# Attention with a gated linear branch and a routed feed-forward layer: softmax weights normalised over four heads at once in the first two chunks of each group

## The reference, cut to what matters

```
scores = jnp.einsum('bqhd,bkhd->bhqk', sq, sk) * scale
scores = jnp.where(causal[None, None], scores, jnp.finfo(scores.dtype).min)
attn = jax.nn.softmax(scores, axis=-1)
y = jnp.einsum('bhqk,bkhd->bqhd', attn, sv)
o = 0.5 * y + 0.5 * o_gla
```

## Time and profile before

| what | us |
|---|---|
| median of three unprofiled runs (lowest, highest) | 944.18 (944.08, 945.03) |
| the profiled execution | 935.75 |
| its span, first to last instruction | 933.5 |
| TensorE matmul busy | 895.2 |
| TensorE weight load busy | 706.8 |
| VectorE busy | 679.4 |
| ScalarE busy | 663.2 |
| GpSimd busy | 635.4 |

### The profile page before, as it was taken

One profiled execution on the slowest core, in us unless ns is written; L12 is line 12 of the kernel. 1 busy time (PEld: TensorE's weight loads), 2 busy tenths in 40 slices (PEclk: granted clock), 3 DMA queues, 4 the chain that ended last, 5 costly groups with the idle time before them and its releaser, 6 DMA issues.

```text
span 933.5 us, 18329 instructions
## 1 busy us (share of the span) xinstructions
PE 895.2 (96%) x5145; PEld 706.8 (76%) x5145; DVE 679.4 (73%) x2010; ACT 663.2 (71%) x2147; POOL 635.4 (68%) x603
## 2 busy tenths in 40 slices
PE   7899999999999999999999999999999989799996
PEld 4577878777777777778788878787776766598885
DVE  5877877676767676767676978877888967475457
ACT  6687777777777777777686877778767767354656
POOL 6967676767566666768676767877656898546441
PEclk9999999999999999999999999999999999999999
DMA  7100100000000000620000001000003111125355
GB/s 266 35 12 29 29 24 1 6 13 7 1 0 0 0 0 7 178 62 1 1 1 2 1 1 44 1 1 17 17 17 106 40 61 41 57 86 148 109 149 202
DMA packets 30969, 41.46 MB, mean 44 GB/s; under 512 B 3230, under 2 KB 25631, under 8 KB 30624
## 3 DMA queue, kind: packets, MB, share of 16 engines
q1 hardware_dynamic: 27472, 31.98, 11.4%
q0 software_dynamic: 3408, 8.43, 2.5%
HBM read 24.72 MB, written 16.59 MB: 44 GB/s over the span
## 4 chain that ended last, share of the span: by engine, by line
PE 77%; DVE 9%; ACT 5%; POOL 4%; issue 3%; DMA 1%; DVEq 0%; POOLq 0%; ACTq 0%
PE PR L518 12%; PE OA L631 12%; PE S L585 10%; PE MS L604 8%; PE S L613 7%; PE OA L593 5%; PE OA L624 4%; PE S L731 3%; PE OA L748 3%; PE PR L564 3%; PE PR L558 3%; POOL slot_x L1717 1%; ACT eqk L879 1%; PE MS L547 1%; DVE pr L1111 1%
## 5 line engine op out<-in xcount | busy, mean ns | idle before, releaser
L1644 POOL TENSOR_TENSOR qd<-eqk,eg 128x512 f32<-128x512 f32 x63 | 75.0, 1190 | 132.3 <-issue 127.6
L631 PE MATMUL OA<-wT,V 128*128 128x512 f32 x320 | 148.4, 594 | 0.0
L841 ACT ACTIVATE S<-S,nm 128x128 f32<-128x128 f32 (+3 forms) x256 | 126.4, 494 | 6.6 <-DVE nm L1077 5.8
L1077 DVE CUSTOM_DVE_ANT_0 S<-S,maskb 128x128 f32<-128x128 f32 (+3 forms) x256 | 118.2, 518 | 13.0 <-PE S L585 11.8
L879 ACT ACTIVATE eqk<-qkv,nmx 128x128 f32<-128x128 f32 x320 | 124.3, 396 | 4.5 <-DVE nmx L1152 4.4
L1632 POOL TENSOR_TENSOR eqk<-eqk,rse 128x640 f32<-128x640 f32 x63 | 79.5, 1263 | 60.1 <-DVE rse L1195 37.0
L631 PEld LDWEIGHTS OA<-wT,V 128*128 128x128 f32 x320 | 59.8, 191 | 69.7 <-issue 69.7
L1111 DVE TENSOR_TENSOR pr<-S,rl 128x256 f32<-128x256 f32 (+3 forms) x128 | 105.5, 825 | 4.5
L1621 POOL TENSOR_TENSOR rp<-qkv,cos 128x640 f32<-128x640 f32 x64 | 99.5, 1555 | 6.8 <-ACT qkv L869 5.8
L1624 POOL TENSOR_TENSOR rp<-rp,rt 128x640 f32<-128x640 f32 x64 | 99.4, 1553 | 5.0
L1621 POOL TENSOR_TENSOR rt<-qkv,sin 128x640 f32<-128x640 f32 x64 | 99.4, 1552 | 0.0
(11 more groups left out here) (259 smaller groups left out, 2443.4 us busy)
## 6 DMA issues: line engine op xcount, KB each, us to landing
qkv<-slot_x SPq DMA_DIRECT2D x39, 129.0 KB, 2.1
slot_x<-zero SPq DMA_DIRECT2D x3, 1290.0 KB, 15.3
stage<-in_wgu SPq DMA_DIRECT2D x8, 352.0 KB, 3.1
stage<-in_wqkv SPq DMA_DIRECT2D x6, 384.0 KB, 3.7
xraw<-in_x_cols SPq DMA_DIRECT2D x16, 128.0 KB, 2.4
acc<-in_x_rows SPq DMA_DIRECT2D x1, 2048.0 KB, 11.1
dn_w<-in_wdn SPq DMA_DIRECT2D x1, 2048.0 KB, 8.2
pr<-plane SPq DMA_DIRECT2D x8, 256.0 KB, 3.9
```

Of the source, the lines that this page charges most:

```text
L631: last = pe.matmul(OA[:, :], V[:, j, :], wT[:, j, :], start=(c == 0 and j == 0), stop=(j == c))
L841: nc.scalar.activation(S[:, h, 0:n], S[:, h, 0:n], ACT.Exp, bias=nm[:, h:h + 1], scale=-1.0, accum_out=ls[:, h:h + 1]).then_inc(s_exp, 1)
L1077: nc.vector.tensor_tensor_reduce(out=S[:, h, 0:n], in0=S[:, h, 0:n], in1=maskb[:, N - n:N], scale=-1.0, scalar=FAR, op0=ALU.add, op1=ALU.m ...
```

## The change

Chunks 0 and 1 of each group use a new function in place of the two calls; chunks 2 and 3 keep them. The new function waits for all four exponentials, takes four reciprocals in one instruction and multiplies all four heads in one instruction of 4n columns (512 at c = 0, 1024 at c = 1). The semaphores are raised by 2 at once, so that all other counts stay. At c = 0 `clamp_gates` now comes ahead of the whole normalisation, since it stood between the pairs.

```
+            def normalise_all(g, c):
+
+                u = C * g + c
+                n = P128 * (c + 1)
+                dve.wait_ge(s_exp, 4 * u + 4)
+                nc.vector.reciprocal(rl[:, :], ls[:, :]).then_inc(s_rl, 2)
+                dve.wait_ge(s_rl, 2 * u + 2)
+                later(dve, s_pt, 10 * g + tri(c))
+                nc.vector.tensor_tensor(pr[:, :, 0:n], S[:, :, 0:n], rl[:, :].rearrange("p (h o) -> p h o", o=1)
+                                        .to_broadcast([P128, GQ, n]), ALU.mult).then_inc(s_pn, 2)
...
                 if n1 and clamp_first:
                     clamp_gates(g, c + 1)
-                normalise(g, c, 0)
+                if c > 1:
+                    normalise(g, c, 0)
                 if n1 and not clamp_first:
                     clamp_gates(g, c + 1)
-                normalise(g, c, 1)
+                if c > 1:
+                    normalise(g, c, 1)
+                else:
+                    normalise_all(g, c)
                 mask_gla(g, c)
```

## The result

The changed kernel is slower: 952.68 us (median of 4 runs, 952.09 to 954.07) against 944.61 us for before (4 runs, 944.08 to 946.15). The ratio is 1.0084, 95% interval 1.0070 to 1.0098, so about 8 us. I forecast 949.1 us with a range up to 952.5: the direction and the place were right, the size was too small by 3 us, and the time is 0.2 us outside the range.

What follows compares the result with a forecast made beforehand. TensorE was taken as the bound, with `pr` arriving last at c = 1: six steps times 0.53 plus four times 0.44 us is 4.9, added to 944.18 gives 949.1 us, range 945.8 to 952.5.

Steps and rivals of the forecast that it cites:

- Bound: TensorE bounds the kernel; at L613 `pr` comes last in 13 of 16 c = 1 steps, with 2.3 us room at c = 0.
- (9, 1), (10, 1) and (12, 1): Steps at c = 1 where TensorE has 0.45 us of room before L613; claimed loss nothing.
- Durations: VectorE's new products: 691 ns at c = 0 for two of 425, 1224 ns at c = 1 for two of 691.
- VectorE's saving: VectorE has 0.27 us less in 32 steps; rival: all 8.6 us reach the end, 935.6 us, chance 0.06.
- What stands behind the last exponential: At c = 1 the whole product follows it: L613 0.53 us later in steps like (1, 1), 0.44 like (8, 1).
- The hand-over: VectorE at c = 1: reciprocal starts 0.05 us after the row sum, product 0.19 later; `pr` 0.46 to 0.53 us later.
- What follows in VectorE's list ... is late by the same amount, so nothing catches up inside the step: Work behind `pr` at c = 1, on VectorE and after TensorE's transposes, shifts by the same 0.44 or 0.53 us.
- Group 13: Its c = 1 step was classed like (1, 1): 0.53 us lost on TensorE, which waits for `pr`.
- Group 11: Its c = 1 step was classed like (8, 1): 0.44 us lost at TensorE's load of L613.
- Groups 0, 14, 15: Their c = 1 delay was taken as zero, absorbed by TensorE's waits for GpSimd (0, 14) or rows (15).
- Nothing gives back: Rival: all 16 steps at c = 1 lose 0.53 us, 8.5 us in all, 952.7 us; chance 0.12, or more loss.

Runs made afterwards that it cites:

- e1_chunk0: The kernel before with the new one-product function at c = 0 alone: ratio 1.0005, 945.42 against 945.07 us.
- e2_chunk1: The kernel before with the new one-product function at c = 1 alone: ratio 1.0094, 954.11 us.
- e7_two_products: The changed kernel with its one wait and one reciprocal kept, but the product in two instructions of two heads: ratio 1.0096, 954.72 us.
- e5_both: The changed kernel with both semaphores raised by 1 and GpSimd made to wait for `gl`: ratio 1.0041, 949.36 against 945.61 us for before.
- e3_by_one: The changed kernel with the normalisation's two semaphores raised by 1 and counts adapted: no gain shown by the runs, 1.5 us less in the trace.
- e9_chunk3: The kernel before with the one product over four heads at c = 3 alone, semaphores raised by 1: ratio 1.0019, 938.83 against 936.82 us.

## Why the prediction was wrong in size, point by point

- **Bound.** Right: at c = 1 `pr` comes last at L613, at c = 0 it has 2 us of room. `e1_chunk0` and `e2_chunk1` put all of the loss in c = 1. In (9, 1), (10, 1) and (12, 1) the room was 0.44 us as read, but `pr` was 0.6 us later.
- **Durations.** Right: 692 and 1225 ns for the new products (I took 691 and 1224), and VectorE's saving was 9.2 us for 8.6.
- **What stands behind the last exponential.** The mechanism was right and is shown by `e7_two_products` and `e5_both`: without the two costs below, L613 starts 0.54 us later in (1, 1) and 0.47 in (8, 1), and their groups are 0.56 and 0.44 us longer, against 0.53 and 0.44 forecast.
- **The hand-over, a mis-sized term.** I gave the new instructions the starts of the old ones. An increment by 2 makes each 0.07 us later: `pr` 0.60 to 0.67 us later than before, not 0.46 to 0.53. It is worth 1.5 us by the traces, 2.0 where GpSimd's meeting is out of the way (6.1 to 4.1 in the table, 951.69 to 949.36 us in the runs of the same rounds).
- **"What follows in VectorE's list ... is late by the same amount, so nothing catches up inside the step": the step that failed.** It holds only if all engines move together. GpSimd did not move with VectorE, and VectorE was pushed into its next instruction: 0.5 us more in five groups, 2.2 us by the traces (8.3 to 6.1). In the runs it is 2 us (1.0084 to 1.0063, in different rounds, intervals that overlap a little) and 3.0 us against `e7_two_products` in the same rounds (1.0096 to 1.0063, intervals apart). I had 4.9 and looked for further losses in waits alone, not in durations. The profile showed the sign: `gl` took 0.51 us in (1, 1) and 0.28 in (8, 0). The step failed the other way round too: in groups 13 and 14 something did catch up inside the step. By the traces the account closes: 4.9 us forecast, less 0.5 in group 13 and 0.3 in group 11, is the 4.1 of `e5_both`; with 2.0 for the increments (0.6 of it in group 11) and 2.2 for the meetings in the five groups it is the 8.3 of the changed kernel.

The Trainium skill (SBUF — State Buffer, Who interferes with whom) says that a VectorE instruction with two SBUF inputs contends with a GpSimd instruction that reads SBUF, and calls the port pair that they share an exclusive lock. The traces agree: 0.29 us free, 1.05 to 1.08 us behind GpSimd, ending 0.15 us after it. It belonged in the forecast, for every instruction that changes its time.

- **Group 13**, which I counted at 0.53, paid nothing, for the same reason. Behind `pr` in (13, 1) VectorE has the routing's L1260 and L1262, a product and an addition of SBUF tiles, beside GpSimd's rotation. Before and after the change:

```profile
674.02 1.10 DVE L1260 TENSOR_TENSOR rk<-rk,tri 128x256 f32<-128x256 f32 x1
675.15 1.67 DVE L1262 TENSOR_TENSOR rk<-rk 128x256 f32<-128x256 f32 x1
...
673.26 1.57 POOL L1621 TENSOR_TENSOR rt<-qkv,sin 128x640 f32<-128x640 f32 x1
674.91 1.62 POOL L1624 TENSOR_TENSOR rp<-rp,rt 128x640 f32<-128x640 f32 x1
```

```profile
683.44 0.42 DVE L1271 TENSOR_TENSOR rk<-rk,tri 128x256 f32<-128x256 f32 x1
683.89 1.65 DVE L1273 TENSOR_TENSOR rk<-rk 128x256 f32<-128x256 f32 x1
...
682.01 1.55 POOL L1636 TENSOR_TENSOR rt<-qkv,sin 128x640 f32<-128x640 f32 x1
683.63 1.63 POOL L1639 TENSOR_TENSOR rp<-rp,rt 128x640 f32<-128x640 f32 x1
```

Before, the first of the two took 1.10 us, as it was held until GpSimd's product had ended at 674.83. In the changed kernel VectorE comes to it 0.7 us later relative to GpSimd, needs only 0.42 us, and ends again 0.3 us after that product: the delay is gone. The second is held until GpSimd's addition ends in both (676.53 and 685.26), and VectorE leaves it with a shift of 8.72 us, GpSimd's own, which is what all had before (13, 1). The kernels with the long product at c = 1 all show this; it was not tried with GpSimd's part left out.
- **Group 11** paid 0.7 us in the changed kernel and 0.1 us with increments by 1, for 0.44 forecast. In (11, 1) two routing comparisons of VectorE, each with its operands in SBUF, meet the rotation's addition on GpSimd. The first of them, and that addition, in the changed kernel and in `e3_by_one`:

```profile
583.72 1.77 DVE L1264 TENSOR_TENSOR rk<-lg 128x256 f32<-128x256 f32 x1
...
583.61 1.60 POOL L1639 TENSOR_TENSOR rp<-rp,rt 128x640 f32<-128x640 f32 x1
```

```profile
583.24 0.42 DVE L1264 TENSOR_TENSOR rk<-lg 128x256 f32<-128x256 f32 x1
...
583.25 1.81 POOL L1639 TENSOR_TENSOR rp<-rp,rt 128x640 f32<-128x640 f32 x1
```

With increments by 1 the first slips through and the second is held for 1.78 us, as before the change. In the changed kernel the first is held, and the second (0.61 us) and `gl` (0.60) still come behind it. So a shift of 0.1 us decides over 0.6 us here.
- **Groups 0, 14, 15.** Group 14 paid nothing, as forecast, but not for the reason that I gave, so this zero was luck. The delay of 0.67 us was gone at L613 of (14, 2), long before TensorE's wait for GpSimd in (15, 0), which I had said would be some 0.5 us shorter and which was 2.25 us for 2.38 (2.31 in the second profile of before). It went as in group 13, at a routing instruction in (14, 1) that had been held beside GpSimd's rotation; before and after the change:

```profile
727.01 0.85 DVE L1358 TENSOR_SCALAR onehot<-rank 128x96 f32<-128x96 f32 x1
```

```profile
736.38 0.20 DVE L1369 TENSOR_SCALAR onehot<-rank 128x96 f32<-128x96 f32 x1
```

In both it ends 0.1 us after GpSimd's product (727.86 and 727.78; 736.58 and 736.49), and GpSimd's shift between the two is 8.7 us, VectorE's on arrival 9.4.

Group 15: `pr` was 0.69 us later in (15, 1), and TensorE's wait for the rows fell from 4.36 to 3.69 us, which takes up most of it. In group 0 the profiles of before differ by 0.4 us among themselves, so its 0.27 us says nothing.
- **The rivals.** VectorE's saving did not reach the end; its point of decision, a second reciprocal that is late by more than the added product time, fits `e9_chunk3`, where 0.53 us of lateness took half of the added 1.07; no run had more lateness than added time. "Nothing gives back" had the right time, 952.7, and the wrong mechanism: groups 13 to 15 did give back. The section on the TRN2 errata of the Trainium skill (VectorE: DVE Perf Modes), which the prediction cites beside the first rival, speaks of operations that read from SBUF, while the wide operand here is read from PSUM; the saving of a merged instruction rests on the rows alone.

## What to carry to other kernels

Before two instructions are merged, ask what releases each: a saved fixed cost counts nothing if the first half was done while the second half's input was still being made, and the merge pays only where the engine is behind by more than the columns that it adds to the end. When an instruction moves in time, look at what the other engine on its port is doing at the new time, not only at its waits. Where several semaphore counts are bent to fit a change, raise them by one and adapt the counts.

## What the runs showed of the hardware

- An instruction of VectorE that raises a semaphore by 2 started 67 ns later after its releaser than one that raises it by 1: the reciprocal after 100 ns in all 32 steps against 33, the product after 270 ns in 30 of 32, against 200 (reciprocal of two columns) to 213 ns (of four). In `e7_two_products`, where only the reciprocal raises by 2, only the reciprocal is late.
- A VectorE instruction of 0.28 us with two SBUF operands took 1.05 to 1.20 us beside a GpSimd product, and an addition of 128x256 took 1.65 to 1.67 us where a product of the same size took 0.42 free. An instruction that is held this way ends at a time that GpSimd sets (`gl` 0.15 us after GpSimd's in all five groups), so an earlier start is lost: `gl` of (1, 1) starts 0.13 us earlier relative to GpSimd in `e3_by_one` and takes 1.20 us for 1.08.
- The expert part of the same kernel differs between executions by about 8 us (spans 933.5 and 942.4 us), and so do its runs from one set of rounds to another (medians of before 945.07 and 936.82 us, both on record for chip 10). In the two profiles of before the difference arises between 840 and 860 us: TensorE waits 3.1 and 4.1 us at L748, and the granted clock of this stretch is 0.74 against 1.00. What lies behind it stays open.
